# A graph convolution on TensorE: each 64th chunk of gathered rows fetched row by row by SyncE

## What is computed

```python
seg = dst * R + edge_type                     # R = 65
sums = segment_sum(x[src], seg).reshape(N, R, 128)
agg  = sums / maximum(count_of(seg), 1.0)
conv = einsum('nri,rio->no', agg, W_rel) + x @ W_root + bias
h    = conv + x @ W_res + b_res
h    = relu((h - mean(h, 0)) * rsqrt(var(h, 0) + EPS) * gamma + beta)
out  = layernorm(x + h)                       # per row, float32
```

## Time and profile before

| | |
|---|---|
| median of 3 runs | 2405.14 us (2402.76 to 2405.75) |
| span of the profiled execution | 2403.0 us |
| between the span and the median | 2.1 us; no time of its own is given for the profiled execution |
| mean granted TensorE clock | 0.935 |
| TensorE busy | 2051.2 us, 85% |
| GpSimd busy | 1485.5 us, 62% |
| VectorE busy | 1396.7 us, 58% |
| ScalarE busy | 886.1 us, 37% |
| DMA | 233.86 MB, 97 GB/s in the mean |

### The profile page before, as it was taken

One profiled execution on the slowest core, in us unless ns is written; L12 is line 12 of the kernel. 1 busy time (PEld: TensorE's weight loads), 2 busy tenths in 40 slices (PEclk: granted clock), 3 DMA queues, 4 the chain that ended last, 5 costly groups with the idle time before them and its releaser, 6 DMA issues.

```text
span 2403.0 us, 38063 instructions
## 1 busy us (share of the span) xinstructions
PE 2051.2 (85%) x13396; PEld 1898.7 (79%) x13396; DVE 1396.7 (58%) x2444; ACT 886.1 (37%) x1651; POOL 1485.5 (62%) x1582
## 2 busy tenths in 40 slices
PE   5798888888888889889888889888988988888987
PEld 3687878878778878877888778777887877778887
DVE  7575565565556556547557457556556555645645
ACT  4333334333333333333333333333333333333333
POOL 6666666666666666666666666666666666666640
PEclk9999989899999989999989989999999989998999
DMA  8643434444443444444343444443343444343433
GB/s 273 162 90 89 96 88 91 94 90 91 94 93 88 90 96 89 90 96 90 88 97 86 91 95 91 91 96 87 89 96 89 90 92 90 88 91 88 91 69 108
DMA packets 244737, 233.86 MB, mean 97 GB/s; under 512 B 27097, under 2 KB 239491, under 8 KB 243907
## 3 DMA queue, kind: packets, MB, share of 16 engines
q0 software_dynamic: 223056, 203.79, 38.1%
q1 hardware_dynamic: 21491, 27.60, 3.7%
HBM read 218.48 MB, written 12.80 MB: 96 GB/s over the span
## 4 chain that ended last, share of the span: by engine, by line
PE 79%; issue 10%; DVE 4%; another core or an unknown queue 3%; ACT 2%; POOL 1%; DMA 1%; ACTq 0%; DVEq 0%; SPq 0%; POOLq 0%
PE tb L667 39%; PE ps L632 29%; PE ps L636 6%; PE tb L560 4%; DVE onehot L1018 2%; ACT agg L770 2%; POOL wsb L515 1%; DVE same L957 1%; DMA wsb<-in_x_dram,srcT 0%; DVE lst L1206 0%; DMA eth<-in_edge_type_dram 0%; PE tb L610 0%; DVE agg L1230 0%; PE tb L580 0%
## 5 line engine op out<-in xcount | busy, mean ns | idle before, releaser
L525 POOL DMA_INDIRECT xg<-xtab,srcT x1545 | 1458.5, 944 | 824.5 <-issue 359.5
L1018 DVE TENSOR_SCALAR onehot<-iota,segT,vT 128x456 fp32r<-128x456 f32 x1563 | 1086.7, 741 | 673.2 <-PE ps L636 423.4
L770 ACT ACTIVATE agg<-ps 128x390 f32 (+1 forms) x1563 | 842.0, 539 | 1454.7 <-PE ps L636 924.2
L667 PE MATMUL tb<-agg,wsb 128*128 128x138 f32 x6370 | 1212.4, 314 | 181.9 <-issue 140.7
L632 PE MATMUL ps<-onehot,xg 128*128 128x390 f32 (+1 forms) x3126 | 1195.2, 447 | 67.1 <-issue 55.9
L667 PEld LDWEIGHTS tb<-agg,wsb 128*128 128x128 f32 x6370 | 921.6, 202 | 219.8 <-issue 170.4
L632 PEld LDWEIGHTS ps<-onehot,xg 128*128 128x128 f32 x3126 | 626.6, 202 | 117.0 <-issue 103.6
L636 PEld LDWEIGHTS ps<-onehot,xg 128*128 128x128 f32 x3028 | 613.8, 203 | 56.8 <-issue 52.8
L636 PE MATMUL ps<-onehot,xg 128*128 128x66 f32 x3028 | 610.5, 202 | 35.9 <-issue 34.2
L957 DVE SCALAR_TENSOR_TENSOR same<-ps,rel 128x1088 bf16<-128x1088 f32 (+3 forms) x96 | 145.5, 1515 | 0.0
L560 PE MATMUL tb<-same,identb 128*128 128x512 bf16 x416 | 114.4, 400 | 26.5 <-DVE same L957 24.9
(11 more groups left out here) (133 smaller groups left out, 338.2 us busy)
## 6 DMA issues: line engine op xcount, KB each, us to landing
xg<-xtab,srcT POOLq DMA_INDIRECT x1545
xtab<-agg SPq DMA_DIRECT2D x4, 1536.0 KB
hinit<-H SPq DMA_DIRECT2D x1, 3125.0 KB
agg<-in_x_dram SPq DMA_DIRECT2D x4, 768.0 KB, 7.5
out_dram<-agg SPq DMA_DIRECT2D x6, 448.0 KB, 3.0
dsth<-in_dst_dram SPq DMA_DIRECT2D x23, 64.0 KB
eth<-in_edge_type_dram SPq DMA_DIRECT2D x23, 64.0 KB
srcr<-in_src_dram SPq DMA_DIRECT2D x12, 64.0 KB
```

The source lines that it names most:

```text
L525: pool.indirect_dma_start(out=xg[c % RING][:], out_offset=None, in_=xtab.bitcast(F32R), in_offset=bass.IndirectOffsetOnAxis(ap=srcT[t % 2] ...
L667: ins = nc.tensor.matmul(o, wsb[:, r * F:(r + 1) * F], pair_rhs(p, r), start=(r == 0), stop=(r == R - 1))
L770: nc.scalar.activation(agg_group(g)[:, :, bass.ds(off, n)], ps[c % NRB][:, 0:n * R].rearrange("f (n r) -> f r n", r=R), ACT.Copy).then_inc ...
L1018: nc.vector.tensor_scalar(onehot[o][:].rearrange("p (a b) -> p a b", a=3), iota3[:, :, 0:IW], segT[t % 2][:, k:k + 1], vT[t % 2][:, k:k + ...
```

## The change

24 chunks, 73, 137, and so on each 64th up to 1545, are no longer gathered by GpSimd. SyncE copies their 24 x 128 source indices straight from HBM into a small tile `spsrc`, one chunk to a partition, with two DMAs that it issues behind the first weight load. After the one-hot of chunk 3 VectorE waits for both copies and multiplies the tile by 1024, which makes byte offsets. SyncE then fetches each such chunk with 128 DMAs of one row of 1024 bytes, loading 16 offsets at a time into registers, into one of two buffers `xsp`. The first fetch stands in SyncE's list behind the store of `hinit`. From the third fetch on SyncE waits first until TensorE has done the chunk after the one that used the buffer before. The row loads of tiles 2 to 12 are placed between the fetches. GpSimd's ring of 18 runs over the remaining 1521 chunks after the first 18; TensorE waits for a fetched chunk on a semaphore that counts 16 for each row, and reads that buffer, for the chunk and for the carry of the next.

```diff
+SP_FIRST = 73
+SP_STEP = 64
+SP_REGS = 16
+SP_OFFS = 3
...
+    ROWB = 4 * 2 * F
+    tab_bytes = xtab.rearrange("n f -> (n f)").bitcast(U8)
...
+    by_sp = list(range(SP_FIRST, NCH, SP_STEP))
+    NSP = len(by_sp)
+    in_ring = [c for c in range(NCH) if c not in by_sp]
+    ring_of = {c: i for i, c in enumerate(in_ring)}
...
+        spsrc = sb("spsrc", [NSP, P], I32)
+        xsp = [sb(f"xsp{s}", [P, 2 * F], F32R) for s in range(2)]
...
         def rows_in_sbuf(c):
-            return xg[c % RING]
+            if c in ring_of:
+                return xg[ring_of[c] % RING]
+            return xsp[by_sp.index(c) % 2]
...
+            whole = SP_STEP * (NSP - 1)
+            sp.dma_start(spsrc[0:NSP - 1, :], src[SP_FIRST * P:(SP_FIRST + whole) * P].rearrange(
+                "(a k e) -> a k e", k=SP_STEP, e=P)[:, 0, :]).then_inc(sp_src, 16)
+            sp.dma_start(spsrc[NSP - 1:NSP, :], src[by_sp[-1] * P:(by_sp[-1] + 1) * P].rearrange("(a e) -> a e", a=1)).then_inc(sp_src, 16)
             sp.wait_ge(raw_free, 1)
             load_rows(1)
...
-            for t in range(2, NTL):
-                sp.wait_ge(raw_free, t)
-                load_rows(t)
+            def fetch_chunk(a):
+                s = a % 2
+                if a == 0:
+                    sp.wait_ge(sp_off, 1)
+                    sp.wait_ge(tab_out, 16 * 3)
+                    sp.wait_ge(tab_rest, 16 * 2)
+                if a >= 2:
+                    sp.wait_ge(agg_ps, by_sp[a - 2] + 2)
+                for e in range(0, P, SP_REGS):
+                    starts = registers(spsrc[a:a + 1, e:e + SP_REGS], ENG.SP, (N - 1) * ROWB)
+                    for k in range(SP_REGS):
+                        sp.dma_start(xsp[s].bitcast(U8)[e + k:e + k + 1, :],
+                                     tab_bytes[bass.ds(starts[k], ROWB)].rearrange("(a b) -> a b", a=1)
+                                     ).then_inc(sp_in[s], 16)
+
+            t = 2
+            for a in range(NSP):
+                while t < NTL and by_sp[a] >= (t - 2) * TC + DVE_SEG + 2 * SP_STEP + 12:
+                    sp.wait_ge(raw_free, t)
+                    load_rows(t)
+                    t += 1
+                fetch_chunk(a)
...
-                pool.wait_ge(agg_ps, c - RING + 2)
+                if c not in ring_of:
+                    continue
+                i = ring_of[c]
+                pool.wait_ge(agg_ps, in_ring[i - RING] + 2)
                 pool.indirect_dma_start(
-                    out=xg[c % RING][:], out_offset=None, in_=xtab.bitcast(F32R),
-                    in_offset=bass.IndirectOffsetOnAxis(ap=srcT[t % 2][:, k:k + 1], axis=0)).then_inc(gath[c % RING], 16)
+                    out=xg[i % RING][:], out_offset=None, in_=xtab.bitcast(F32R),
+                    in_offset=bass.IndirectOffsetOnAxis(ap=srcT[t % 2][:, k:k + 1], axis=0)).then_inc(gath[i % RING], 16)
...
+                elif c in ring_of:
+                    pe.wait_ge(gath[ring_of[c] % RING], 16 * (ring_of[c] // RING + 1))
                 else:
-                    pe.wait_ge(gath[c % RING], 16 * (c // RING + 1))
+                    a = by_sp.index(c)
+                    pe.wait_ge(sp_in[a % 2], 16 * P * (a // 2 + 1))
...
                 one_hot(c)
+                if c == SP_OFFS:
+                    dve.wait_ge(sp_src, 32)
+                    nc.vector.tensor_scalar(spsrc[:], spsrc[:], float(ROWB), None, ALU.mult).then_inc(sp_off, 1)
```

More of the change, by code:

```diff
@@ L11 @@
 I32 = mybir.dt.int32
+U8 = mybir.dt.uint8
 ALU = mybir.AluOpType
@@ L105, in pair_len @@
         return min(GC, NCH - p * GC)
+    by_sp = list(range(SP_FIRST, NCH, SP_STEP))
+    NSP = len(by_sp)
+    assert SP_FIRST > RING and NCH - by_sp[-1] > 0 and P % SP_REGS == 0
+    in_ring = [c for c in range(NCH) if c not in by_sp]
+    ring_of = {c: i for i, c in enumerate(in_ring)}
     def row_loads(t):
@@ L265, in gnn @@
         agg_ps = sem("agg_ps")
+        sp_src = sem("sp_src")
+        sp_off = sem("sp_off")
+        sp_in = [sem(f"sp_in{s}") for s in range(2)]
         evac = sem("evac")
@@ L432, in _ @@
             sp.dma_start(hinit, H[:, 0:N]).then_inc(hinit_out, 16)
-            for t in range(2, NTL):
-                sp.wait_ge(raw_free, t)
-                load_rows(t)
+            def fetch_chunk(a):
[19 more added lines that the diff above has]
+                fetch_chunk(a)
+            assert t == NTL
             def fast():
```

## The result

| | before | after |
|---|---|---|
| median, same chip | 2403.95 us (2400.01 to 2405.75, 4 runs) | 2441.28 us (2438.85 to 2442.97, 4 runs) |
| span of the profiled execution | 2403.0 | 2439.1 |
| mean granted clock of TensorE | 0.935 | 0.928 |

The ratio is 1.0159, with a 95% interval of 1.0144 to 1.0173, so +37 us. The forecast was 2420, +15 on its own scale. Sign and range hold, the size is less than half.

The account below looks back on a forecast made before the run. The prediction took TensorE as the bound (busy 85% of the span). Its terms: 2403.0 + 9 + 5.7 + 1.7 = 2419.4 us, 2421.5 on the median's scale, given as 2420; range 2408 to 2452, the forecast's own 2410 to 2430.

Parts of the forecast that it names:

- Second: the rate of SyncE: SyncE's fetches before chunk 73: at 72 us each, the first is late by 5.7 us, once; later ones keep up.
- T: Time SyncE needs to fetch one chunk: 72 us taken, between 41 and 100.
- the first stall: VectorE waits at chunk 3 for the index copies, so TensorE starts chunk 4 late: 9 us, bounds 0 to 12.
- the second stall: TensorE waits before chunk 73 for the first fetch, late once: 5.7 us.
- its clock: TensorE's clock after the stall before chunk 73: 3.4 us at a granted clock of 0.50, 1.7 us lost, charged once.
- What the change removes: worth nothing: 24 gathers fewer on GpSimd, hidden in its waits for TensorE: taken as 0, bounds 0 to -30 us.
- Fourth: DMA load. Cost 0, bound 0 to 3: Fetched rows add at most 17% DMA load; gathers land fractions of a microsecond later: cost 0, bound 0 to 3.
- SyncE as the bound: Rival: a fetch takes over 94.5 us and SyncE sets the pace: 2445 to 2576 us, chance 0.17.
- a late fetch of 14 to 28 us: Rival: fetches take 80 to 94 us, giving one stall of 14 to 28 us: 2430 to 2445, chance 0.15.
- no stall: Rival: indices land early or TensorE's wait from 69 to 74 us takes up the delay: 2405 us, chance 0.11.
- The faster rival: Rival: gathers are on the path and TensorE's unnamed gaps are waits for them: 2375 us at most, chance 0.04.

Follow-up runs that it names:

- no_stalls: The changed kernel with VectorE's byte offsets made after chunk 20 and fetches begun at chunk 137 (23 chunks): 2421.43 us, ratio 1.0071 of the kernel before.
- unread: The kernel before, but from chunk 72 on gathers land in four spare buffers that TensorE neither waits for nor reads: ratio 1.006.
- block_load: load_only with each fetch made by one DMA of 128 contiguous rows, the same 128 KB: ratio 1.0011.
- fixed_rows: load_only with fixed addresses: 128 DMAs of one row a fetch, without register loads or MOVEs: ratio 1.0137.
- by_eight: fixed_rows with 16 DMAs of 8 contiguous rows a fetch in place of 128 DMAs of one: ratio 1.0024.
- rows_alone: fixed_rows without any gather from chunk 72 on: 1870.49 us, ratio 0.7785.
- load_only: no_stalls with GpSimd gathering all chunks and the 23 fetches going into buffers that nobody reads: 2449.12 us, ratio 1.018.
- skip_only: no_stalls with only the first two fetches made; the 23 gathers stay away and TensorE reads old rows for the others: 2382.27 us, ratio 0.9902.
- static_rows: The kernel before, but from chunk 72 on one SyncE DMA of 128 contiguous rows replaces each gather, TensorE waiting as before: 1870.19 us, ratio 0.7657.
- half_count: The kernel before, but from chunk 72 on each gather fetches 64 rows in place of 128: ratio 1.0015.
- half_rows: The kernel before, but from chunk 72 on each gather takes rows of 512 B in place of 1024 B: ratio 0.9993.

## Why the prediction was right in sign and too small

**"Second: the rate of SyncE", T = 72 us: near, by luck in part.** The first fetch took 75.3 us with its 8 register loads. One fetch was late, SyncE did not become the bound, and TensorE waited for xsp once. The parts were not as predicted: a register load takes 1165 ns in the median, and the eight of the first fetch took 9.3 us together, in place of 2.8; that leaves 0.52 us a row (66 / 128) in place of 0.54, 3 us less.

**The stalls: right in place, a little small.** For the first stall the prediction had 9 us; the start of chunk 4 slipped by 11.1, and removing the stall gave back 10.2. The slip was 13.9 by chunk 18, which TensorE reached partly at the clock of 0.50, a loss that the prediction had put at nothing for this stall; 10.3 at chunk 23, ahead of which TensorE sits idle for 1.72 us where it sat for 4.70 before, so that part is caught up; and 14.3 at chunk 72. The mis-sized term is the landing of the second copy, 55.1 predicted; VectorE went on at 57.1, 3.8 us after that copy was issued at 53.3, where I took 1.8 from a gather in an empty system. For the second stall and its clock the prediction had 5.7 + 1.7 = 7.4 us; no_stalls gave back 9.7, of which some 0.8 belongs to the one fetched chunk less (17.4 / 23), so 8.9. TensorE waited 7.9 us where 5.7 were predicted: T was 3.3 longer, of which the first register load, 3.16 us, makes nearly all, and chunk 73 was wanted 68.5 us after the store of hinit and not 67.3. The clock was as charged: 3.4 us at 0.50 after the stall, as in the earlier trace rows.

**"What the change removes: worth nothing": failed.** 23 gathers fewer are worth 25.7 us, 1.1 each. The bound of 30 us was there, and I took its other end, since no gather is late. That TensorE's loss is no wait for gathers holds: unread shows a TensorE that waits for none and isn't faster. But a gather has another price than its lateness.

**"Fourth: DMA load. Cost 0, bound 0 to 3": failed, the larger error.** 23 fetches cost 45 us, so 24 cost 47. I had sized the load by packets and share of time, and by that measure it is next to nothing: SyncE's queue moved 6170 packets more, not 98,000, and its share went from 3.7 to 4.2% (block_load, with the same bytes, costs 1.0011). The price goes by the number of DMAs and exists only beside gathers (fixed_rows, by_eight, rows_alone).

The sum in the prediction's terms: 10.2 + 8.9 for the stalls (16.4 predicted) and 24 x (17.4 / 23) = 18.2 for the exchange (0 predicted) make 37.3; measured, 37.2 on the first series' base. These are differences of the same four kernels, so the agreement is no test; the test is that load_only and skip_only, made independently, add up to 19.3 against 17.4.

**The rivals.** SyncE as the bound, a late fetch of 14 to 28 us, no stall: none came. The faster rival said that TensorE's unnamed gaps belong to gathers. They do, but as a disturbance and not as waits for rows, and its point, the time between issue and use falling to the landing time, is the wrong test. It had found the right money, 30 us, and missed that the fetches cost more than that.

**The rule of the Trainium skill** in the prediction (page "DMA: Bandwidth & Descriptors", section "Issuing engines are not separate DMA queues": that spreading DMAs over issuing engines saves the issuer's time alone) doesn't cover these runs. With the same packets, bytes and DMA share, SyncE's plain DMAs in place of GpSimd's indirect ones made a difference of 573 us of TensorE time (static_rows). The page speaks of the issuer alone, and the form of the DMA changed with it, so this is no clean test of its sentence.

**What stays open.** What it is in GpSimd's indirect DMA that TensorE feels. It is not the bytes, the number or place of the rows, the wait, or GpSimd's being busy with fills. Issuer, indices and element type were not changed one at a time, and no view here tells what TensorE does in a gap. The same page of the Trainium skill, in its section "SWDGE vs HWDGE vs iDMA", says that GpSimd's DMAs get their descriptors from software, in rings in SBUF, while SyncE's come from hardware. The runs agree that the two kinds differ; that the rings are the cause is not shown, and half_count, with 43% fewer packets and the same time, speaks against their volume. Nor is it known why one gather left out in 64 gives 1.1 us and all left out give 0.38 each, or by what route SyncE's DMAs add to the disturbance. In the profiled executions the 610 chunks of fixed_rows that overlapped a fetch took some 36 us longer than the same chunks in half_rows (same chip, ratio 0.9993 of before), the 869 others from chunk 137 on 2 us less, with 20 and 26 us of scatter: that hints at a cost while the DMAs are issued, and shows no more. Nor do the runs split the other 0.4% of load_only (itself hardly clear of noise) between register loads, MOVEs and the longer fetch.

## What to carry to other kernels

A DMA off the path can still tax the engine on it: before you call a transfer free, time the kernel with the transfer left out and with its result unread. If TensorE shows gaps of some 0.4 us labelled "issue" while GpSimd gathers, test the gathers as a cost by themselves: here leaving them out took 23% off the time, though the last gather's rows lay ready 18 us ahead of need. And beside such gathers a replacement by many small DMAs is priced by their number, not by their bytes.

## What the runs showed of the hardware

- One GpSimd indirect DMA a chunk kept TensorE from running gapless: medians of 2402 to 2443 us with, 1869 to 1871 us without, on the four chips that ran both. The whole difference between these chips lies in the time with gathers.
- One SyncE DMA of 128 rows, 1491 times, cost TensorE nothing that shows, contiguous (1870.19 us against 1869.79 without any rows, on another chip) or with rows 48 KB apart (1869.19).
- 2944 one-row DMAs of SyncE cost 31 to 33 us beside gathers (fixed_rows) and nothing that shows without them (rows_alone, 1870.49 us).
- A load of 16 registers on SyncE took 1165 ns in the median, and 3158 the first time, right behind the issue of a large store; a load of 4 on ScalarE took 308.
